# Turning the ternary down-weight pieces by DMA in place of TensorE

## The chip, the cores and the metric

The kernel runs on one core of a Trainium2 chip. The metric is the device time of one execution in microseconds (us); a kernel's time is the median of several runs. The profile is of one further execution.

## The reference

Four conditioned sequences of 1024 rows of 512 numbers pass through two layers. The first quantises its activations and its down weights:

```python
scale = cond @ norm_w.T + 1.0
h = x * (scale[:, None, :] * rsqrt(mean(x * x) + EPS))
val, gate = split(h @ up_w.T)                  # up_w: 4096 x 512
h = val * gelu(gate)                           # 2048 wide
hq = round(h * 127 / max|h|) * max|h| / 127    # per row
wq = clip(round(down_w / mean|down_w|), -1, 1) * mean|down_w|   # down_w: 512 x 2048
x1 = hq @ wq.T + x
```

The second layer is a bottleneck of 128 whose two weight matrices are built from the condition: `x1 + relu(x1 @ Wd_b.T + bd) @ Wu_b.T + bu`, with `Wd_b = Wd + 0.1 * (cond @ Wdd.T + bdd)` and `Wu_b` alike.

## The kernel before

The 4096 rows are worked in eight chunks of 512. A chunk has 16 iterations j. In each, TensorE (PE) multiplies one gate tile (12 matmuls of 128x512, three for each of four slices of the 512 inputs: high by high, high by low and low by high half of a split float, L947 to L949) and one value tile of the same size. ScalarE (ACT) applies Gelu to the gate tile (L545), VectorE (DVE) multiplies it by the value tile (L797), ScalarE takes the absolute value (L556) and VectorE a running maximum (L734). From the next chunk on, the 16 tiles of the chunk before are scaled and rounded (L706, L522, L525), and in iterations 9 to 12 PE does the down products with `wqT`, the turned ternary weights (L1000). Beside this the condition's big matrices stream through (loads L299, turned on VectorE by L724, multiplied by PE at L959). After the eight chunks the second layer follows.

Chunk 0 also prepares the weights. Every engine runs its own list of instructions in the order written, and semaphores join them. In iteration j of chunk 0:

- **SP** issues all DMAs, one after another: `load_up(j + 4)` (two loads of up weights, L278), in j = 7 and 8 `turn_x`, which turns the next chunk's rows by DMA transposes from SBUF to SBUF (L269 for the high half, L271 for the low half, each 128x512 of a 2-byte type), `load_pieces(j - 6)` for j = 7 to 13 (L292; it waits until the piece before in the same buffer is quantised), in j = 11 three loads `load_nat` of 512 KB (L299) and from j = 13 one each.
- **PE** does the gate tile (it waits for `w_lo_done`, L1023, that is, for `w_lo_half(j)` on VectorE), `turn_w(j + 2)` (8 transposes in float32 of the up weights, L924; waits for `w_scaled`), the value tile, and for j >= 8 `turn_pieces(j - 8)` (L933 to L940).
- **ACT** does Gelu(j), `w_hi_half(j + 2)` (L510), `w_square(j + 3)` (L504), the absolute value, for j = 7 to 14 the two pieces' scaling and rounding (L569), and for j >= 8 `copy_pieces(j - 8)` (L513), which converts eight turned blocks to fp8 in `wqT` (L516).
- **DVE** does the maximum of j - 1 (L734), from j = 13 a unit of `turn_nat` (L724), `w_lo_half(j + 2)` (L665), the product (L797), `w_exponents(j + 3)` (L641 to L651), `w_scale(j + 3)` (L658), and for j = 7 to 14 `quant_pieces(j - 7)`: clip both pieces (L711), wait until the pair before has been turned (L713), then write both to `piece_q`, a bfloat16 view of `s_bc` (L716).

The down weights go through in 16 pieces of 128x512, two at a time: the pair i is loaded in SP's iteration i + 6, rounded and clipped in iteration i + 7 and turned and converted in iteration i + 8. The turned blocks lie in the PSUM bank TA, whose uses are counted by `ta_full` and `ta_freed`; TA also serves the row of scales (L496). The first use of `wqT` is in chunk 1, iteration 9 (L993). With the first iteration of chunk 1 PE turns the running maximum of chunk 0 (L984, after the gate tile; it waits for all 16 maxima), and before its gate tile it waits for 15 products (`h_done`, L1019).

Of the kernel before, what the change touches and what calls it, by code (L numbers as in the profile page):

```python
# [7 lines left out]
BF16 = mybir.dt.bfloat16  # L8
# [3 lines left out]
ACT = mybir.ActivationFunctionType  # L12
AX = mybir.AxisListType

P = 128
# [7 lines left out]
def conditioned_block(nc, x, cond, norm_w, up_w, down_w, Wd, bd, Wu, bu, Wdd, bdd, Wdu, bdu, out):  # L23
# [9 lines left out]
    FT = FF // P  # L33
# [14 lines left out]
    with ExitStack() as ctx:  # L48
        def sb(name, shape, dt):
            return ctx.enter_context(nc.sbuf_tensor(name, shape, dt))  # L50

        def sem(name):
            return ctx.enter_context(nc.semaphore(name))
# [4 lines left out]
        w_hi = w_hi_reg[:, :].bitcast(F16).rearrange("p (k f) -> p k f", k=KD)  # L58
        w_lo = w_lo_reg[:, :].bitcast(F16).rearrange("p (k f) -> p k f", k=KD)
        wqT = sb("wqT", [P, FT, D], F8)  # L60
        base_wd = sb("base_wd", [P, KD * BN], F32)
        base_wu = sb("base_wu", [P, D], F32)

# [67 lines left out]
        def piece_q(p):  # L131
            return s_bc[:, :].bitcast(BF16)[:, (p % 2) * 512:(p % 2 + 1) * 512]
# [10 lines left out]
        def x_bank(k):  # L143
# [28 lines left out]
        piece_in = [sem(f"piece_in{i}") for i in range(2)]  # L172
        piece_biased, piece_quant, mean_step, base_done = (sem(n) for n in (
            "piece_biased", "piece_quant", "mean_step", "base_done"))
        x0_in = [sem(f"x0_in{t}") for t in range(TT)]
        x_in, x_squared, ms_done, x_rstd, x_scaled = sem("x_in"), sem("x_squared"), sem("ms_done"), sem("x_rstd"), sem("x_scaled")
        ta_full, ta_freed, x_hi_done, x_lo_done, x_turned = (sem(n) for n in (
# [23 lines left out]
        TA_BASE = KD  # L201
        TA_SC = TA_BASE + 2
        TA_MEAN = TA_SC + 1
        TA_PIECE = TA_MEAN + 1
        TA0 = TA_PIECE + FT // 2


        def squares_in(c, j):
# [49 lines left out]
        def _(sp):  # L258
# [26 lines left out]
            def load_pieces(i):  # L285
                for p in (2 * i, 2 * i + 1):
                    if i == 0 and p == 0:
                        sp.wait_ge(ta_full, TA_BASE + 2)
                    if i > 0:
                        sp.wait_ge(piece_quant, 4 * (i - 1) + 3 + p % 2)  # L290
                    dt, fb = p // 4, p % 4
                    sp.dma_start(piece(p), down_w[dt * P:(dt + 1) * P, fb * 512:(fb + 1) * 512]).then_inc(piece_in[p % 2], 16)  # L292

            def load_nat(u):
                m, t = u // 4, u % 4
                src = (Wdd, Wdu)[m % 2].rearrange("(a u p e) h -> u p a (e h)", a=2, p=P, e=4)[4 * (m // 2) + t]
                if u >= NAT:
                    sp.wait_ge(nat_turned, u - NAT + 1)
                sp.dma_start(nat[:, u % NAT, :, :], src).then_inc(nat_in[u % NAT], 16)  # L299
# [43 lines left out]
            def run(c, par, b):  # L343
                first, last = is_first(c), b is None
                for j in range(FT):
                    if first and j < FT - 4:
                        load_up(j + 4)
                    if not last and not first and j == 1:
                        load_x(c + 1)
                    if not last:  # L350
                        for t in turns_in(c, j):
                            turn_x(c + 1, t)
                    if last and j == 4:
                        sp.wait_ge(x_turned, 32 * TT * c)
                        load_x1(0, 0)
                        sp.wait_ge(val_full, FT * c)
                        load_x1(1, 1)
                    if first and j == 4:
                        load_rows(3)
                        load_pieces(0)  # L360
                    if first and 7 <= j < 14:
                        load_pieces(j - 6)
                    if first and j == 11:
                        for u in range(NAT):
                            load_nat(u)
                    for u in units_at(c, j):
                        if u + NAT < UNITS:
                            load_nat(u + NAT)
                    if not first:
                        if j in (7, 8):  # L370
                            load_xr(c - 1, j - 7)
                        if 10 <= j < 10 + TT:
                            store_x1(c - 1, j - 10)
                        if j in (11, 12):
                            load_xr(c - 1, j - 9)
                    for m in batch_at(c, j):
                        if m % 2 == 1:
                            store_stage(m)
                    if last and j == 6:
                        load_deltas()  # L380
# [90 lines left out]
        def _(act):  # L471
# [40 lines left out]

            def copy_pieces(i):  # L513
                dt, f0 = i // 2, 8 * (i % 2)
                act.wait_ge(ta_full, TA_PIECE + i + 1)
                act.activation(wqT[:, f0:f0 + 8, dt * P:(dt + 1) * P],  # L516
                               TA[:, :].bitcast(BF16).rearrange("p (f d) -> p f d", f=8), ACT.Copy, saturate=False).then_inc(ta_freed, 1)

            def round_pair(c, k0):
                for k in (k0, k0 + 1):  # L520
# [116 lines left out]
        def _(dve):  # L637
# [70 lines left out]
            def quant_pieces(i):  # L708
                for p in (2 * i, 2 * i + 1):
                    dve.wait_ge(piece_biased, p + 1)  # L710
                    dve.tensor_scalar(piece(p), piece(p), ROUND + 1.0, ROUND - 1.0, ALU.min, ALU.max).then_inc(piece_quant, 1)  # L711
                if i > 0:
                    dve.wait_ge(ta_full, TA_PIECE + i)  # L713
                for p in (2 * i, 2 * i + 1):
                    dve.wait_ge(piece_quant, 4 * i + 1 + p % 2)
                    dve.tensor_scalar(piece_q(p), piece(p), ROUND, None, ALU.subtract).then_inc(piece_quant, 1)  # L716
# [195 lines left out]
        def _(pe):  # L912
# [17 lines left out]
                    mm = pe.transpose(TA[:, k * P:(k + 1) * P], sc[:, k, b:b + 1].to_broadcast([P, P]), identf[:, :])  # L930
                mm.then_inc(ta_full, 1)

            def turn_pieces(i):  # L933
                pe.wait_ge(piece_quant, 4 * i + 4)
                pe.wait_ge(ta_freed, TA_PIECE + i)
                for p in (2 * i, 2 * i + 1):
                    for a in range(4):
                        o = (4 * (p % 2) + a) * P
                        mm = pe.transpose(TA[:, :].bitcast(BF16)[:, o:o + P], piece_q(p)[:, a * P:(a + 1) * P], identb[:, :])
                mm.then_inc(ta_full, 1)  # L940

            def up_products(par, ft, bank, done, x_waits=False):
                cols = slice(ft * P, (ft + 1) * P)
                for k in range(KD):
# [47 lines left out]

            def down_products(c, t):  # L993
                if t == 0:
                    pe.wait_ge(ta_freed, TA0)
                    pe.wait_ge(q_done, FT * (c + 1))
                if t > 0:
                    pe.wait_ge(y_done, TT * c + t)
                for f in range(FT):
                    mm = pe.matmul(Y[:, :], q[:, f, t * P:(t + 1) * P], wqT[:, f, :], start=(f == 0), stop=(f == FT - 1))  # L1000
                mm.then_inc(y_full, 1)
# [12 lines left out]
            def run(c, par, b):  # L1014
# [5 lines left out]
                for j in range(FT):  # L1020
# [31 lines left out]
                        spread_scales(c - 1)  # L1052
                    if row_in(c, j):
                        spread_row(b)
                    if first and j >= 8:
                        turn_pieces(j - 8)
                    if not first and 9 <= j < 9 + TT:
                        down_products(c - 1, j - 9)

# [119 lines left out]
```

## Time and profile before

| what | value |
|---|---|
| median of 3 runs | 972.29 us (970.92 to 973.04) |
| the profiled execution | 972.11 us |
| its span | 970.3 us |
| PE busy | 952.5 us (98%) |
| DVE busy | 667.7 us (69%) |
| ACT busy | 432.3 us (45%) |
| granted TensorE clock, mean over the span | 0.998 |
| DMA queues, share of 16 engines | 48.9% |

The profiled execution lies 0.18 us under the median, and what lies around its span is 1.8 us. "Busy" counts the time in which an engine executes; a matmul of 128x512 is shown as 380 ns, but the next begins 0.22 us after it, so neighbours overlap.

### The profile page before, as it was taken

The page shows a single profiled execution, that of the slowest core. Times are in us where ns is not written, and L with a number is a line of the kernel's source. Part 1 is how long each engine was busy: PE and PEld are TensorE (multiplying, and loading weights), DVE is VectorE, ACT ScalarE, POOL GpSimd, SP SyncE. Part 2 cuts the span into 40 slices and gives each one's busy share as a digit, 9 for nine tenths or more (in the row PEclk, how much of TensorE's full clock was granted, in tenths as well). Part 3 has the DMA queues.
Part 4 walks back from the last instruction along what each step waited for, and adds up shares of the span by engine and source line. Part 5 has one row for each costly group of instructions (what it writes and reads, how often), then busy time and mean ns, then how long its engine had stood idle before and what let it go on. Part 6 is the DMA issues. An engine that isn't in the chain of part 4 may idle for free.

```text
span 970.3 us, 13569 instructions
## 1 busy us (share of the span) xinstructions
PE 952.5 (98%) x5248; PEld 456.0 (47%) x5248; DVE 667.7 (69%) x1053; ACT 432.3 (45%) x795; POOL 52.1 (5%) x52
## 2 busy tenths in 40 slices
PE   7999999999999999999999999999999999999998
PEld 5545544444444444444444444444444444445453
DVE  6769877866877577857886687857787584236333
ACT  5778767322752157213742266214741265117121
POOL 1000000000000000000000000000000000000554
PEclk9999999999999999999999999999999999999999
DMA  9445543564436643573347643764346632210674
GB/s 328 149 136 169 176 151 98 150 186 113 160 109 175 172 131 98 152 194 127 119 129 177 150 132 101 176 163 141 120 141 154 162 131 72 81 55 22 237 239 175
DMA packets 103769, 141.93 MB, mean 146 GB/s; under 512 B 35732, under 2 KB 41368, under 8 KB 103192
## 3 DMA queue, kind: packets, MB, share of 16 engines
q1 hardware_dynamic: 103704, 141.06, 48.9%
q8 instruction: 41, 0.67, 0.3%
q14 instruction: 24, 0.20, 0.1%
HBM read 112.72 MB, written 20.97 MB: 138 GB/s over the span
## 4 chain that ended last, share of the span: by engine, by line
PE 94%; DVE 2%; DMA 2%; ACT 1%; issue 1%; SPq 0%; DVEq 0%; ACTq 0%
PE bank L947 22%; PE bank L948 22%; PE bank L949 22%; PE bank L1000 10%; PE bank L959 6%; PE bank L1121 3%; PE bank L1134 3%; DMA xn<-in_x 2%; PE bank L1010 1%; PE bank L1112 1%; PE bank L924 1%; PE bank L984 0%; PE bank L990 0%; DVE h L797 0%; ACT h L576 0%
## 5 line engine op out<-in xcount | busy, mean ns | idle before, releaser
L947 PE MATMUL bank<-x_split,w_hi 128*128 128x512 f16 x1024 | 389.1, 380 | 2.3 <-DVE x_split L676 2.3
L948 PE MATMUL bank<-x_split,w_hi 128*128 128x512 f16 x1024 | 388.9, 380 | 0.0
L949 PE MATMUL bank<-x_split,w_lo 128*128 128x512 f16 x1024 | 388.7, 380 | 0.0
L724 DVE STREAM_TRANSPOSE delta_reg<-delta_reg 128x512 f32<-128x512 f32 x256 | 261.0, 1110 | 12.9 <-PE bank L959 12.9
L556 ACT ACTIVATE g<-h 128x512 f32<-128x512 f32 x128 | 80.7, 630 | 271.2 <-DVE h L797 271.2
L797 DVE SCALAR_TENSOR_TENSOR h<-bank,desc,g 128x512 f32<-128x512 f32 x128 | 94.5, 738 | 113.1 <-issue 88.9
L545 ACT ACTIVATE g<-bank,desc 128x512 f32<-128x512 f32 x128 | 87.7, 685 | 164.0 <-PE bank L949 163.8
L947 PEld LDWEIGHTS bank<-x_split,w_hi 128*128 128x128 f16 x1024 | 100.4, 98 | 128.3 <-issue 11.1
L949 PEld LDWEIGHTS bank<-x_split,w_lo 128*128 128x128 f16 x1024 | 100.4, 98 | 121.2 <-issue 0.7
L948 PEld LDWEIGHTS bank<-x_split,w_hi 128*128 128x128 f16 x1024 | 100.4, 98 | 112.1 <-issue 0.8
L1000 PE MATMUL bank<-wqT,qreg 128*128 128x512 fp8e4 x448 | 101.3, 379 | 0.0
L734 DVE TENSOR_TENSOR absrun<-absrun,g 128x512 f32<-128x512 f32 x120 | 82.4, 686 | 24.5 <-ACT g L556 23.7
L706 DVE TENSOR_TENSOR h<-h,s_bc 128x512 f32<-128x512 f32 x112 | 71.7, 681 | 2.0 <-ACT s_bc L529 2.0
L1000 PEld LDWEIGHTS bank<-wqT,qreg 128*128 128x128 bf16 x448 | 43.8, 98 | 52.9
L752 DVE SCALAR_TENSOR_TENSOR xr<-bank,fy,xr 128x512 f32<-128x512 f32 x30 | 22.4, 751 | 66.5 <-DMA xr<-in_x 28.6
L522 ACT ACTIVATE h<-h 128x512 f32<-128x512 f32 x112 | 64.4, 621 | 5.3 <-DVE h L706 5.3
L525 ACT ACTIVATE qreg<-h 128x512 bf16<-128x512 f32 x112 | 63.6, 616 | 0.0
L959 PE MATMUL bank<-delta_reg,cond_diag 128*32 128x256 f32 x1024 | 61.9, 382 | 0.0
L888 DVE TENSOR_TENSOR w_hi<-bank,w_hi 128x512 f32<-128x512 f32 x32 | 21.9, 690 | 39.9 <-PE bank L1134 39.6
L446 POOL TENSOR_TENSOR rstd<-ss,mhalf 128x4 f32<-128x4 f32 x8 | 10.7, 1334 | 691.3 <-DVE ss L670 691.3
L959 PEld LDWEIGHTS bank<-delta_reg,cond_diag 128*32 128x32 f32 x1024 | 30.0, 109 | 30.0 <-issue 13.6
L1134 PE MATMUL bank<-delta_reg,w_lo 128*128 128x512 f32 x64 | 30.5, 609 | 1.3 <-ACT w_lo L608 0.8
(133 smaller groups left out, 558.1 us busy)
## 6 DMA issues: line engine op xcount, KB each, us to landing
delta_reg<-in_L_cond_Wdd SPq DMA_DIRECT2D x64, 512.0 KB, 3.8
delta_reg<-in_L_cond_Wdu SPq DMA_DIRECT2D x64, 512.0 KB, 3.8
qreg<-in_L_cond_up_w SPq DMA_DIRECT2D x32, 256.0 KB, 4.3
xr<-in_x SPq DMA_DIRECT2D x30, 256.0 KB, 4.3
x_scratch<-xr SPq DMA_DIRECT2D x30, 256.0 KB, 4.7
xn<-in_x SPq DMA_DIRECT2D x7, 1024.0 KB, 6.3
out_y<-w_hi SPq DMA_DIRECT2D x7, 1024.0 KB, 4.8
h<-in_L_cond_down_w SPq DMA_DIRECT2D x4, 1024.0 KB, 7.9
```

What stands on the lines that cost most here:

```text
L522: act.activation(h[:, k, :], h[:, k, :], ACT.Copy, bias=ROUND).then_inc(round_added, 1)
L545: act.activation(g[:, j % 2, :], GATE[j % 2][:, :], ACT.Gelu, scale=desc[:, 2 * j + 1:2 * j + 2]).then_inc(gelu_done, 1)
L556: act.activation(g[:, j % 2, :], h[:, j, :], ACT.Abs).then_inc(abs_done, 1)
L706: dve.tensor_tensor(h[:, k, :], h[:, k, :], s_bc[:, :], ALU.mult).then_inc(h_scaled, 1)
L724: last = dve.transpose(natT[:, t, kk, :, :].rearrange("p a (r e) -> p e a r", e=4), nat[:, u % NAT, kk, :])
L734: dve.tensor_tensor(absrun[:, :], absrun[:, :], g[:, j % 2, :], ALU.max).then_inc(max_done, 1)
L797: dve.scalar_tensor_tensor(h[:, j, :], VAL[j % 2][:, :], desc[:, 2 * j:2 * j + 1], g[:, j % 2, :], ALU.mult, ALU.mult).then_inc(h_done, 1)
L947: pe.matmul(bank[:, :], w_hi[:, k, cols], xh[:, par, k, :], start=(k == 0), stop=False)
L948: pe.matmul(bank[:, :], w_hi[:, k, cols], xl[:, par, k, :], start=False, stop=False)
L949: mm = pe.matmul(bank[:, :], w_lo[:, k, cols], xh[:, par, k, :], start=False, stop=(k == KD - 1))
L959: mm = pe.matmul(HY[32 * t:32 * t + 32, cols], cond_diag[:, a, :], natT[:, (4 * m + t) % NATT, :, a, :], start=(a == 0), stop=(a == HB - 1))
L1000: mm = pe.matmul(Y[:, :], q[:, f, t * P:(t + 1) * P], wqT[:, f, :], start=(f == 0), stop=(f == FT - 1))
```

## The change

The eight PE instructions of each `turn_pieces(i)` are taken out of PE's list. In their place SP issues, in its iteration i + 8, ahead of `load_pieces`, two DMA transposes, each of one 128x512 bfloat16 piece from `piece_q` into the new SBUF buffer `pieceT` (2 KB a partition). They wait for the pieces to be quantised and, from the second pair on, for ScalarE to have converted the pair before (`wq_done`), as `pieceT` holds one pair. ScalarE's conversion reads `pieceT` in place of TA and waits for both transposes. VectorE's wait in `quant_pieces`, with which it spares `piece_q` until it has been read, is now for the transposes to have landed. The uses of TA are renumbered.

```diff
--- before.py
+++ after.py
@@ -58,6 +58,7 @@
         w_hi = w_hi_reg[:, :].bitcast(F16).rearrange("p (k f) -> p k f", k=KD)
         w_lo = w_lo_reg[:, :].bitcast(F16).rearrange("p (k f) -> p k f", k=KD)
         wqT = sb("wqT", [P, FT, D], F8)
+        pieceT = sb("pieceT", [P, 2, 4, P], BF16)
         base_wd = sb("base_wd", [P, KD * BN], F32)
         base_wu = sb("base_wu", [P, D], F32)
 
@@ -172,6 +173,7 @@
         piece_in = [sem(f"piece_in{i}") for i in range(2)]
         piece_biased, piece_quant, mean_step, base_done = (sem(n) for n in (
             "piece_biased", "piece_quant", "mean_step", "base_done"))
+        piece_turned, wq_done = sem("piece_turned"), sem("wq_done")
         x0_in = [sem(f"x0_in{t}") for t in range(TT)]
         x_in, x_squared, ms_done, x_rstd, x_scaled = sem("x_in"), sem("x_squared"), sem("ms_done"), sem("x_rstd"), sem("x_scaled")
         ta_full, ta_freed, x_hi_done, x_lo_done, x_turned = (sem(n) for n in (
@@ -201,8 +203,7 @@
         TA_BASE = KD
         TA_SC = TA_BASE + 2
         TA_MEAN = TA_SC + 1
-        TA_PIECE = TA_MEAN + 1
-        TA0 = TA_PIECE + FT // 2
+        TA0 = TA_MEAN + 1
 
 
         def squares_in(c, j):
@@ -290,6 +291,13 @@
                         sp.wait_ge(piece_quant, 4 * (i - 1) + 3 + p % 2)
                     dt, fb = p // 4, p % 4
                     sp.dma_start(piece(p), down_w[dt * P:(dt + 1) * P, fb * 512:(fb + 1) * 512]).then_inc(piece_in[p % 2], 16)
+
+            def turn_pieces(i):
+                for p in (2 * i, 2 * i + 1):
+                    sp.wait_ge(piece_quant, 4 * i + 3 + p % 2)
+                    if i > 0:
+                        sp.wait_ge(wq_done, i)
+                    sp.dma_start(pieceT[:, p % 2, :, :], piece_q(p), transpose=True).then_inc(piece_turned, 16)
 
             def load_nat(u):
                 m, t = u // 4, u % 4
@@ -358,6 +366,8 @@
                     if first and j == 4:
                         load_rows(3)
                         load_pieces(0)
+                    if first and j >= 8:
+                        turn_pieces(j - 8)
                     if first and 7 <= j < 14:
                         load_pieces(j - 6)
                     if first and j == 11:
@@ -512,9 +522,9 @@
 
             def copy_pieces(i):
                 dt, f0 = i // 2, 8 * (i % 2)
-                act.wait_ge(ta_full, TA_PIECE + i + 1)
+                act.wait_ge(piece_turned, 32 * (i + 1))
                 act.activation(wqT[:, f0:f0 + 8, dt * P:(dt + 1) * P],
-                               TA[:, :].bitcast(BF16).rearrange("p (f d) -> p f d", f=8), ACT.Copy, saturate=False).then_inc(ta_freed, 1)
+                               pieceT[:, :, :, :].rearrange("p a f d -> p (a f) d"), ACT.Copy, saturate=False).then_inc(wq_done, 1)
 
             def round_pair(c, k0):
                 for k in (k0, k0 + 1):
@@ -710,7 +720,7 @@
                     dve.wait_ge(piece_biased, p + 1)
                     dve.tensor_scalar(piece(p), piece(p), ROUND + 1.0, ROUND - 1.0, ALU.min, ALU.max).then_inc(piece_quant, 1)
                 if i > 0:
-                    dve.wait_ge(ta_full, TA_PIECE + i)
+                    dve.wait_ge(piece_turned, 32 * i)
                 for p in (2 * i, 2 * i + 1):
                     dve.wait_ge(piece_quant, 4 * i + 1 + p % 2)
                     dve.tensor_scalar(piece_q(p), piece(p), ROUND, None, ALU.subtract).then_inc(piece_quant, 1)
@@ -930,15 +940,6 @@
                     mm = pe.transpose(TA[:, k * P:(k + 1) * P], sc[:, k, b:b + 1].to_broadcast([P, P]), identf[:, :])
                 mm.then_inc(ta_full, 1)
 
-            def turn_pieces(i):
-                pe.wait_ge(piece_quant, 4 * i + 4)
-                pe.wait_ge(ta_freed, TA_PIECE + i)
-                for p in (2 * i, 2 * i + 1):
-                    for a in range(4):
-                        o = (4 * (p % 2) + a) * P
-                        mm = pe.transpose(TA[:, :].bitcast(BF16)[:, o:o + P], piece_q(p)[:, a * P:(a + 1) * P], identb[:, :])
-                mm.then_inc(ta_full, 1)
-
             def up_products(par, ft, bank, done, x_waits=False):
                 cols = slice(ft * P, (ft + 1) * P)
                 for k in range(KD):
@@ -992,7 +993,7 @@
 
             def down_products(c, t):
                 if t == 0:
-                    pe.wait_ge(ta_freed, TA0)
+                    pe.wait_ge(wq_done, FT // 2)
                     pe.wait_ge(q_done, FT * (c + 1))
                 if t > 0:
                     pe.wait_ge(y_done, TT * c + t)
@@ -1052,8 +1053,6 @@
                         spread_scales(c - 1)
                     if row_in(c, j):
                         spread_row(b)
-                    if first and j >= 8:
-                        turn_pieces(j - 8)
                     if not first and 9 <= j < 9 + TT:
                         down_products(c - 1, j - 9)
```

## Rows read from the trace of the kernel before

**Rows 1.** Page, part 1 (busy us, share, instructions) and part 4 (chain).

```profile
PE 952.5 (98%) x5248; PEld 456.0 (47%) x5248; DVE 667.7 (69%) x1053; ACT 432.3 (45%) x795; POOL 52.1 (5%) x52
...
PE 94%; DVE 2%; DMA 2%; ACT 1%; issue 1%; SPq 0%; DVEq 0%; ACTq 0%
```

**Rows 2.** Busy time by stretch: start:end length, busy us by engine, granted clock, DMA.

```profile
131.00:250.00 119.00, 119.00 (x698) 54.74 (x696) 89.40 (x121) 52.05 (x93) 1.38 (x1) 1.00 0.49 143
```

**Rows 3.** Chain that ended last, 80 to 90 us: start, us, what.

```profile
81.13 0.45 PE bank L939 x8
```

**Rows 4.** Timeline of SP's queue, 78 to 107 us: start, us, engine, line, what.

```profile
78.63 0.81 SPq L292 DMA_DIRECT2D qreg<-in_L_cond_down_w  x2
79.49 0.90 SPq L278 DMA_DIRECT2D qreg<-in_L_cond_up_w  x2
...
81.68 1.26 SPq L271 DMA_TRANSPOSE x_split<-xn  x1
...
84.30 1.26 SPq L271 DMA_TRANSPOSE x_split<-xn  x1
85.61 1.05 SPq L292 DMA_DIRECT2D qreg<-in_L_cond_down_w  x2
...
105.14 1.46 SPq L299 DMA_DIRECT2D delta_reg<-in_L_cond_Wdd  x3
```

**Rows 5.** Single DMAs by source line: issue in ns, start; then issue to landing.

```profile
L271 SPq DMA_TRANSPOSE x_split<-xn x1: 1264/1264/1264, 81.7 to 81.7; - x1
...
DMA to landing us min/median/max: 3.7/3.7/3.7
...
L271 SPq DMA_TRANSPOSE x_split<-xn x1: 1264/1264/1264, 84.3 to 84.3; - x1
...
DMA to landing us min/median/max: 2.5/2.5/2.5
...
L299 SPq DMA_DIRECT2D delta_reg<-in_L_cond_Wdd x2: 469/469/469, 105.6 to 106.1; - x2
...
DMA to landing us min/median/max: 5.8/6.2/6.6
```

**Rows 6.** Timeline of DVE, 84 to 124 us.

```profile
84.86 0.76 DVE L716 TENSOR_SCALAR s_bc<-qreg 128x512 bf16<-128x512 f32 x2
...
92.81 1.29 DVE L665 TENSOR_TENSOR w_lo<-bank,w_hi 128x512 f16<-128x512 f32 x2 [0.27 <-ACT w_hi L510]
...
95.76 0.88 DVE L658 TENSOR_SCALAR qreg<-qreg,winv 128x512 f32<-128x512 f32 x2
96.56 0.76 DVE L711 TENSOR_SCALAR qreg<-qreg 128x512 f32<-128x512 f32 x2
...
110.23 0.76 DVE L716 TENSOR_SCALAR s_bc<-qreg 128x512 bf16<-128x512 f32 x2
...
123.64 0.76 DVE L716 TENSOR_SCALAR s_bc<-qreg 128x512 bf16<-128x512 f32 x2
```

**Rows 7.** Timeline of ACT, 84 to 91 us.

```profile
84.39 1.00 ACT L516 ACTIVATE wqT<-bank 128x1024 fp8e4<-128x1024 bf16 x1
...
90.71 1.00 ACT L516 ACTIVATE wqT<-bank 128x1024 fp8e4<-128x1024 bf16 x1
```

**Rows 8.** Timeline of PE, 66 to 130 us.

```profile
69.56 1.09 PE L924 MATMUL bank<-identf,qreg 128*128 128x128 f32 x8 [2.30 <-DVE qreg L658]
...
128.90 0.66 PE L984 MATMUL bank<-identf,absrun 128*128 128x128 f32 x4 [0.98 <-DVE absrun L734]
```

**Rows 9.** Busy time by stretch, the stretch after PE stood at 67 to 69.6 us.

```profile
70.60:74.26 3.66, 3.66 (x12) 1.35 (x11) 3.66 (x7) 3.53 (x8) 0.00 (x0) 0.53 0.19 40
```

**Rows 10.** Page, part 5: 128x512 reads by ScalarE, from SBUF and from PSUM.

```profile
L556 ACT ACTIVATE g<-h 128x512 f32<-128x512 f32 x128 | 80.7, 630 | 271.2 <-DVE h L797 271.2
...
L545 ACT ACTIVATE g<-bank,desc 128x512 f32<-128x512 f32 x128 | 87.7, 685 | 164.0 <-PE bank L949 163.8
```

**Rows 11.** Transposes of L269 over the whole span, issue to landing.

```profile
DMA to landing us min/median/max: 2.5/5.1/6.3
```

## Prediction

> **What bounds the kernel now.** I read the page first: PE is busy 98% of the span and makes up 94% of the chain that ended last [rows 1]. Then the busy time by stretch: from 131 to 250 us PE never stops, at full clock [rows 2]. So what starts PE late at the end of chunk 0 is not made up later; a delay there is a delay of the end. The chain from 80 to 90 us shows the instructions in question on that chain: eight transposes of L939 hold PE for 0.45 us [rows 3]. Last I read the queues beside PE in iterations 8 to 15 of chunk 0, since the change moves the work to SP and puts waits of ScalarE and VectorE behind it. Four readings matter. SP issues without a gap from 79.49 to 86.66 us, a DMA transpose taking 1.26 us of its time [rows 4]. VectorE was ready to write the second pair of pieces at 84.86 us [rows 6], ScalarE to convert the first at 84.39 us [rows 7]. And PE waits there for VectorE's scaled up weights and, at the change of chunk, for its last maximum [rows 8].
>
> **PE's share.** 8 times 0.45 us [rows 3] go, 3.6 us at most. That is what the change can win, if everything else stays hidden. It counts only while PE is what ends last.
>
> **The first pair.** SP reaches `turn_pieces(0)` behind the four transposes of x, at 85.61 us, where `load_pieces(2)` stood [rows 4]. The second transpose is issued at 85.61 + 1.26 = 86.87. The nearest row for its landing is the one issued at 84.30, with no loads ahead of it: 2.5 us [rows 5]. It lands at 89.4. VectorE stands at L713 from 84.86 to 89.4, 4.5 us, and behind this wait are the low halves of the up weights, the product and `w_scale`, which PE needs for its next `turn_w`. ScalarE stands at `copy_pieces(0)` from 84.39 to 89.4, and behind it are the next Gelu and `w_hi_half`. Neither has anything else to do first, so PE stops as well. The 0.45 us that PE saves in each iteration become waiting: from here on my sum follows L716, not PE.
>
> **The loop that then forms.** Landing of pair i - 1, VectorE's first L716 (half of 0.76 us [rows 6], with its signal 0.45), `load_pieces`, `load_up`, two transposes, landing of pair i. The same sequence stands in the trace, with transposes of x: pieces issued at 78.63, up weights at 79.49, the second transpose at 81.68 [rows 4], landed 3.7 us later [rows 5], so 85.38 - 78.63 = 6.75 us from the loads to the landing. The loop takes 6.75 + 0.45 = 7.2 us. The engines' own loop runs from the conversion (90.71 [rows 7]) over w_lo at 92.81 and w_scale at 95.76 to the end of the clipping at 96.56 + 0.76 [rows 6], 6.6 us. 7.2 is the longer, so it is the period for iterations 9, 10 and 11: 89.4, 96.6, 103.8, 111.0 us.
>
> **Iteration 12.** Between its `load_pieces` and `turn_pieces(4)` stand the three 512 KB loads, 1.46 us of issue [rows 4]. The last one landed at 106.1 + 6.6 = 112.7, which is 8.4 us after the piece load at 104.30 [rows 4, 5]. In the sequence of the last part the transposes landed right behind the loads issued ahead of them, so I put the pair 0.5 us behind these: 0.45 + 8.9 = 9.35 us, 120.35 in place of 110.23 [rows 6], 10.1 us late.
>
> **Iterations 13 and 14.** The up weights are finished. The two intervals take 13.4 us before (110.23 to 123.64 [rows 6]); I leave the first as it is, for its transposes follow only the pieces, and add 0.8 us to the second, where one 512 KB load is ahead again (as much data as in the 7.2 us loop). Bounds: nothing, and 2 us. L716 of the last pair: 134.5 in place of 123.64, 10.9 us late. What follows up to PE's turn of the maximum is unchanged: 128.90 [rows 8] becomes 139.8. The last conversion (pair 7) waits for a pair issued at about 135.5, landed about 139.3; it ends behind PE's turn and has chunk 1 to be read in, so it costs nothing.
>
> **ScalarE's conversion.** It keeps its shape and 1.00 us [rows 7], only the source moves from PSUM to SBUF. Of 128x512 the pass from SBUF takes 630 ns, one from PSUM 685 (another function) [rows 10]: between 0.1 us less and 0.1 us more. I take nothing; it lies in the 6.6 us loop, which has 0.6 us to spare.
>
> **The clock.** PE will stand at the end of chunk 0 for over 5 us: its own work would be done by 134, and the maximum comes at 139.8. Before, PE stood for 2.30 us [rows 8], and the 3.66 us that began 1 us after it resumed were granted 0.53, about the lower level of 1.2 GHz [rows 9]. That is 3.66 x 0.47 = 1.7 us lost. After the 0.98 us stop at 128.90 [rows 8] the clock stayed whole. The stop of over 5 us is on PE's path and gets the 1.7 us; the earlier drops fall into waiting time and cost nothing. Bounds: nothing, and twice as much.
>
> **The sum.** 10.9 + 1.7 = 12.6 us. PE's 3.6 us are not subtracted, as they are inside the waits. Against the profiled execution of 972.11 us (span 970.3) this gives 984.7; the median of the runs shown is 0.18 us higher, so 984.9 us.
>
> **A rule beside the rows.** Eight transposes in 0.45 us are 56 ns each on PE [rows 3], and a DMA transpose of four such blocks lands after 2.5 us alone [rows 5]. The Trainium skill, "VectorE: DVE Perf Modes", section "The three transpose paths", gives 390 ns for a 128x128 bf16 transpose on TensorE and 1309 ns through the DMA crossbar. It speaks against the change as I do, but by its figures 64 blocks would free 25 us of PE and a pair of pieces would take 10.5 us to turn; no row here has blocks that slow on either path.
>
> **Rivals.**
> (a) Faster. The mechanism: the pairs land before VectorE and ScalarE come to their waits, and PE's path shrinks by 3.6 us, to 968.7. The place that decides is the first pair: it would have to be issued by 82.4 us to land by 84.86. For it: VectorE and ScalarE are not the bound. Against: SP is held by the x transposes up to 85.61 [rows 4], and nothing in the change moves them. 3 in 100; that waits and gain cancel, 2 in 100.
> (b) The first stop happens, but the loop keeps up. If transposes don't queue behind loads, the second lands 0.85 + 0.9 + 1.26 + 2.5 = 5.5 us after the loads, the loop is 6.0, and the engines' 6.6 sets the period: 89.4 + 3 x 6.6 = 109.2, and the same for iteration 12, 115.8; 5.6 us late. Without the clock's cost 977.9, with it 979.6. Against: in chunk 0 the transpose behind loads took 3.7 us, not 2.5 [rows 5]. 15 in 100.
> (c) The transposes queue worse than in the nearest row. Over the span the median to landing is 5.1 us and the worst 6.3 [rows 11], among the 512 KB loads. With 5.1 in place of 3.7 in each of three loops and one like it for iteration 14, 5.6 us more, 990.5; with 6.3 it is 995. 12 in 100.
> (d) The two transposes of a pair go one after the other instead of overlapping. With 3.7 us each the loop is 0.45 + 1.75 + 7.4 = 9.6; the first pair lands at 85.61 + 5.0 = 90.6, and six loops later it is 148.2 in place of 123.64: 24.6 + 1.7 late, 998.6. Against: transposes issued 1.3 us apart landed well under twice that [rows 4, 5]. 3 in 100. By the 1309 ns of the Trainium skill, "VectorE: DVE Perf Modes", "The three transpose paths", a pair would take 10.5 us, which is this case made sharper: a loop of 12.7 us and a time of some 1020 us.
> The forecast itself has 65 in 100.
>
> **The numbers.** The forecast spreads from 981 to 989 by its bounds (the 3 us of iteration 12, iteration 14, the clock). With most of (b) below and the start of (c) above, 978 to 990 holds 8 in 10. A measurement of this kernel tells about 0.2%, 1.9 us, from no change: faster has 0.03, within it 0.02, slower 0.95.
>
> **What would show it.** First, the first L716 of the second pair: at 89.4, waiting on the DMA into `pieceT`. Second, the intervals between pairs of L716: 7.2, 7.2, 7.2, 9.3 us, and the waits of L516 for the same DMA of about 5 us, then some 0.5 to 3. Third, L984 at 139.8 and a clock of about 0.5 for some 3.5 us behind it. Fourth, from then on every row later by one constant. If L716 comes at 84.9 the first step is wrong; if the intervals are 6.6, it is (b); if L984 is at 125 to 129, it is (a), and I have misjudged the whole direction. If the delay is some 11 us at L984 but less at the end, then PE was not the bound behind it.

## The result and the profile after

| | kernel before | changed kernel |
|---|---|---|
| median | 971.61 us (4 runs, 970.79 to 973.04) | 988.03 us (4 runs, 986.91 to 989.32) |
| profiled execution | 972.11 us, span 970.3 | 988.77 us, span 986.9 |

The ratio is 1.0168, with a 95% interval of 1.0156 to 1.0181: 16.4 us slower. The forecast was 984.9 us, that is 12.6 us slower, within 978 to 990. The lines of the changed kernel are numbered a little higher: L716 is now L726 (`piece_q`), L516 is L526 (ScalarE's conversion), L924 is L934 (`turn_w`), L984 is L985 (the turn of the maximum), L990 is L991 (the turn of the scales), L292 and L278 are L293 and L279 (loads of pieces and of up weights), L299 is L307 (the 512 KB loads), and L300 are the new transposes.

The page of the changed kernel, parts 1 and 4, beside [rows 1]:

```profile
PE 957.7 (97%) x5184; PEld 456.5 (46%) x5184; DVE 667.8 (68%) x1053; ACT 433.1 (44%) x795; POOL 52.1 (5%) x52
...
PE 90%; DVE 3%; DMA 3%; SPq 2%; issue 1%; ACT 1%; DVEq 0%; ACTq 0%
PE bank L948 21%; PE bank L949 21%; PE bank L950 21%; PE bank L1001 10%; PE bank L960 6%; PE bank L1120 3%; PE bank L1133 3%; DMA pieceT<-s_bc 2%; PE bank L1011 1%; PE bank L1111 1%; PE bank L934 1%; SPq L300 1%; DVE w_lo L675 0%; DVE h L80
```

PE is busy for longer in total although 64 instructions are gone (in this stage it ran at the lower clock in two stretches, near 95 and near 143 us, below), and the new DMA is 2% of the chain that ended last. The chain between 84 and 98 us (start, us, what) is the mechanism, link by link:

```profile
84.69 1.27 SPq L272
...
86.01 1.26 SPq L300
...
87.32 2.48 DMA pieceT<-s_bc
...
89.82 0.04 DVE s_bc L726
...
90.65 0.43 SPq L293
...
91.12 0.43 SPq L279
...
92.14 1.19 SPq L300
...
93.43 3.83 DMA pieceT<-s_bc
...
97.28 0.04 DVE s_bc L726
```

SP's transposes of x, then the two new ones, then the landing, then the first write of `piece_q`; this releases the load of the next pieces, behind which come the up weights, the next two transposes and the next landing. No matmul stands in it. SP's timeline, for the first two pairs and for the pair behind the three 512 KB loads, beside [rows 4]:

```profile
86.01 2.57 SPq L300 DMA_TRANSPOSE pieceT<-s_bc  x2
90.28 0.80 SPq L293 DMA_DIRECT2D qreg<-in_L_cond_down_w  x2
91.12 0.90 SPq L279 DMA_DIRECT2D qreg<-in_L_cond_up_w  x2
92.14 2.52 SPq L300 DMA_TRANSPOSE pieceT<-s_bc  x2
...
112.21 0.81 SPq L293 DMA_DIRECT2D qreg<-in_L_cond_down_w  x2
113.07 1.46 SPq L307 DMA_DIRECT2D delta_reg<-in_L_cond_Wdd  x3
114.62 3.50 SPq L300 DMA_TRANSPOSE pieceT<-s_bc  x2
```

VectorE's timeline, the first `piece_q` of a pair each time, beside [rows 6]; in brackets how long it was idle before and for what. The line at 104.01 is the clipping of pair 3:

```profile
89.82 0.76 DVE L726 TENSOR_SCALAR s_bc<-qreg 128x512 bf16<-128x512 f32 x2 [4.48 <-DMA pieceT<-s_bc]
...
97.28 0.76 DVE L726 TENSOR_SCALAR s_bc<-qreg 128x512 bf16<-128x512 f32 x2 [1.01 <-DMA pieceT<-s_bc]
...
101.67 0.75 DVE L807 SCALAR_TENSOR_TENSOR h<-bank,desc,g 128x512 f32<-128x512 f32 x1 [0.95 <-issue]
...
104.01 0.77 DVE L721 TENSOR_SCALAR qreg<-qreg 128x512 f32<-128x512 f32 x2
104.82 0.76 DVE L726 TENSOR_SCALAR s_bc<-qreg 128x512 bf16<-128x512 f32 x2
...
111.76 0.76 DVE L726 TENSOR_SCALAR s_bc<-qreg 128x512 bf16<-128x512 f32 x2 [0.49 <-DMA pieceT<-s_bc]
...
122.54 0.76 DVE L726 TENSOR_SCALAR s_bc<-qreg 128x512 bf16<-128x512 f32 x2 [4.34 <-DMA pieceT<-s_bc]
```
```profile
137.42 0.76 DVE L726 TENSOR_SCALAR s_bc<-qreg 128x512 bf16<-128x512 f32 x2 [1.40 <-DMA pieceT<-s_bc]
```

In the second interval (97.28 to 104.82) VectorE doesn't wait for the landing: its clipping ended at 104.78, and the chain that ended last has the landing at 104.80. It had stood 0.95 us before its product (L807), of which the profile names no cause; PE worked at the lower clock on the value tile that this product reads. So here the landing and the engines' own work ended together.

Who waited for the new transposes (us in all, times), and their issue to landing over all 16:

```profile
  ACT wqT L526: 15.1, 7
  DVE s_bc L726: 11.7, 5
...
DMA to landing us min/median/max: 2.5/3.8/7.4
```

PE's timeline where it stood longest, beside [rows 8], and the busy time, with the granted clock third from the end of the line, beside [rows 9]:

```profile
95.25 1.97 PE L934 MATMUL bank<-identf,qreg 128*128 128x128 f32 x8 [4.65 <-DVE qreg L668]
```
```profile
142.65 1.12 PE L985 MATMUL bank<-identf,absrun 128*128 128x128 f32 x4 [6.12 <-DVE absrun L744]
...
148.58 0.60 PE L991 MATMUL bank<-identf,s 128*128 128x128 f32 x4
```
```profile
142.65:150.00 7.35, 7.35 (x25) 3.65 (x26) 3.39 (x8) 1.99 (x3) 0.00 (x0) 0.60 0.43 134
```

PE stood for 4.65 us near 95 and for 6.12 us before the turn of the maximum, and in the 7.35 us that followed it had 0.60 of the clock: the first matmuls there start 0.43 us apart, as at the lower level, 1.2 GHz, in place of 0.22. From the turn of the maximum to the turn of the scales it took 5.93 us (142.65 to 148.58), where the kernel before needed 3.08 (128.90 to 131.98), of which the second line is

```profile
131.98 0.60 PE L990 MATMUL bank<-identf,s 128*128 128x128 f32 x4
```

So the 16.6 us by which the spans differ are these, counted from the first L716 or L726 (78.18 before, 78.58 after). Two lines of the kernel before on which the intervals rest:

```profile
78.18 0.76 DVE L716 TENSOR_SCALAR s_bc<-qreg 128x512 bf16<-128x512 f32 x2
...
103.85 0.76 DVE L716 TENSOR_SCALAR s_bc<-qreg 128x512 bf16<-128x512 f32 x2
```

| piece | before | after | lost, us | forecast, us |
|---|---|---|---|---|
| start of the span to the first pair | 78.18 | 78.58 | 0.40 | 0 |
| interval to pair 1 (iteration 8) | 6.68 | 11.24 | 4.56 | 4.5 |
| pairs 2, 3 and 4 (iterations 9 to 11) | 18.99 | 21.94 | 2.95 | 2.6 |
| pair 5 (iteration 12, 512 KB loads) | 6.38 | 10.78 | 4.40 | 3.0 |
| pairs 6 and 7 | 13.41 | 14.88 | 1.47 | 0.8 |
| last pair to the turn of the maximum | 5.26 | 5.23 | 0.0 | 0 |
| turn of the maximum to turn of the scales | 3.08 | 5.93 | 2.85 | 1.7 |
| from there to the end | 838.3 | 838.3 | 0.0 | 0 |

### The profile page after: what moved, and what is told of

Read it like the earlier page. It is cut to its first block, busy times and chain, and to the rows that moved or that the text cites. A ratio compares the mean times of both kernels' runs of the same rounds, so it can differ in the third digit from the quotient of the medians.

```text
span 986.9 us, 13463 instructions
## 1 busy us (share of the span) xinstructions
PE 957.7 (97%) x5184; PEld 456.5 (46%) x5184; DVE 667.8 (68%) x1053; ACT 433.1 (44%) x795; POOL 52.1 (5%) x52
## 4 chain that ended last, share of the span: by engine, by line
PE 90%; DVE 3%; DMA 3%; SPq 2%; issue 1%; ACT 1%; DVEq 0%; ACTq 0%
PE bank L948 21%; PE bank L949 21%; PE bank L950 21%; PE bank L1001 10%; PE bank L960 6%; PE bank L1120 3%; PE bank L1133 3%; DMA pieceT<-s_bc 2%; PE bank L1011 1%; PE bank L1111 1%; PE bank L934 1%; SPq L300 1%; DVE w_lo L675 0%; DVE h L807 0%; DMA xn<-in_x 0%
## 5 line engine op out<-in xcount | busy, mean ns | idle before, releaser
L807 DVE SCALAR_TENSOR_TENSOR h<-bank,desc,g 128x512 f32<-128x512 f32 x128 | 94.5, 738 | 111.0 <-issue 86.6
L716 DVE TENSOR_TENSOR h<-h,s_bc 128x512 f32<-128x512 f32 x112 | 71.8, 683 | 4.4 <-ACT s_bc L539 4.4
L532 ACT ACTIVATE h<-h 128x512 f32<-128x512 f32 x112 | 64.4, 622 | 5.3 <-DVE h L716 5.3
```

Source lines behind the costliest of these rows:

```text
L532: act.activation(h[:, k, :], h[:, k, :], ACT.Copy, bias=ROUND).then_inc(round_added, 1)
L716: dve.tensor_tensor(h[:, k, :], h[:, k, :], s_bc[:, :], ALU.mult).then_inc(h_scaled, 1)
L807: dve.scalar_tensor_tensor(h[:, j, :], VAL[j % 2][:, :], desc[:, 2 * j:2 * j + 1], g[:, j % 2, :], ALU.mult, ALU.mult).then_inc(h_done, 1)
```

## The experiments

The theory: the time is lost because VectorE and ScalarE wait for a landing of their own iteration, in a loop that runs through SP's queue; the slow clock after the long stop comes on top; and PE's freed 3.6 us are worth up to 3.6 us. The main rival: SP's 20 us of added issue time and the added traffic cost it, whoever waits. A second one: ScalarE's wait alone makes the loop. "To the maximum" is the time from the first L716 to the turn of the maximum, in the profile of each. The ratio is to the runs of the kernel before that were made beside each kernel; their medians lie between 971.2 and 972.3 us.

| kernel | median us | ratio to before, 95% interval | to the maximum | on to the scales |
|---|---|---|---|---|
| before | 971.6 | 1 | 50.7 | 3.1 |
| changed kernel | 988.0 | 1.0168 (1.0156 to 1.0181) | 64.1 | 5.9 |
| both buffers doubled | 975.6 | 1.0043 (1.0028 to 1.0058) | 54.2 | 3.1 |
| `piece_q` doubled | 985.7 | 1.0146 (1.0131 to 1.0161) | 60.8 | 5.9 |
| `pieceT` doubled | 988.4 | 1.0174 (1.0159 to 1.0189) | 64.4 | 5.7 |
| no turning | 975.7 | 1.0049 (1.0032 to 1.0066) | 52.3 | 4.8 |
| before, with idle transposes | 974.7 | 1.0032 (1.0022 to 1.0042) | 53.5 | 3.1 |
| first pair ahead | 988.0 | 1.0164 (1.0149 to 1.0180) | 65.0 | 5.2 |
| PE kept busy | 984.7 | 1.0127 (1.0112 to 1.0143) | 63.9 | 3.1 |
| 512 KB loads later | 985.3 | 1.0129 (1.0110 to 1.0148) | 61.3 | 5.7 |
| no turning, nobody waits | 972.8 | 1.0010 (1.0001 to 1.0020) | 49.6 | 4.6 |
| the same, PE kept busy | 972.5 | 1.0004 (0.9994 to 1.0013) | 50.7 | 3.0 |
| both doubled, x spread | 974.3 | 1.0025 (1.0014 to 1.0036) | 52.4 | 4.8 |
| the same, PE kept busy | 973.2 | 1.0014 (1.0005 to 1.0024) | 52.3 | 3.0 |

### The waits: both buffers doubled

A second pair of `piece_q` and a second `pieceT` lie in a part of `delta_reg` that nobody uses before chunk 1 (whose first writer waits for the last conversion). Each pair parity has a semaphore of its own.

```diff
-                if i > 0:
-                    dve.wait_ge(piece_turned, 32 * i)
+                if i > 1:
+                    dve.wait_ge(piece_turned[i % 2], 32 * (i // 2))
...
-                    if i > 0:
-                        sp.wait_ge(wq_done, i)
+                    if i > 1:
+                        sp.wait_ge(wq_done, i - 1)
...
-                    if first and j >= 8:
-                        copy_pieces(j - 8)
+                    if first and j >= 9:
+                        copy_pieces(j - 9)
+                    if c == 1 and j == 0:
+                        copy_pieces(7)
```

> The changed kernel with two pairs of piece_q and two of pieceT, the conversion one iteration later: nobody waits for a transpose of the same iteration. My theory (the time is lost in the waits of VectorE and ScalarE for a landing of the same iteration): PE's 3.6 us come through and at most 1 us of loads issued late is lost, 968.0 to 969.5. Rival (SP's queue time and the transposes' traffic cost it): both are still there, so 980 or more.

975.6 us: 12.5 of the 16.4 us are gone with the waits, though every DMA is still issued. But 4 us remain, and the theory's 968.0 to 969.5 is missed by 6 us. ScalarE's timeline in this kernel shows the first of them:

```profile
91.42 0.72 ACT L591 ACTIVATE qreg<-qreg,wtot 128x512 f32<-128x512 f32 x1 [2.33 <-DMA qreg<-in_L_cond_down_w]
93.05 0.72 ACT L591 ACTIVATE qreg<-qreg,wtot 128x512 f32<-128x512 f32 x1 [0.91 <-DMA qreg<-in_L_cond_down_w]
```

It waits 2.33 and 0.91 us for the pieces of pair 2 (L591 is its L569). SP had issued them at 88.19, behind four x transposes and two new ones, where the kernel before issued them at 85.61 [rows 4]. So the rival holds a part: the place in SP's queue.

### The queue and the traffic alone: idle transposes

The kernel before, PE turning as ever, with 16 DMA transposes of spare memory at the places of the new ones.

```diff
+            def idle_turn(i):
+                for p in (2 * i, 2 * i + 1):
+                    sp.wait_ge(piece_quant, 4 * i + 3 + p % 2)
...
+                    sp.dma_start(idle_out[:, p % 2, :, :], idle_in, transpose=True).then_inc(idle_turned[p % 2], 16)
...
+                    if first and j >= 8:
+                        idle_turn(j - 8)
                     if first and 7 <= j < 14:
                         load_pieces(j - 6)
```

> The kernel before, PE still turning, with the changed kernel's 16 DMA transposes at the same places of SP's queue but from and into spare memory, with nobody waiting for them (each only for the one into its place an iteration ago). My theory (waits): SP's 20 us of issue and the traffic cost at most 1.5 us, 971.5 to 973. Rival (queue and traffic): 980 or more.

974.7 us, 3.1 more (interval of the ratio 1.0022 to 1.0042), and 2.8 us more up to the maximum. Twice the 1.5 us that the theory allowed, and well below the rival's 980. The cause is in the same place, ScalarE's wait for pair 2 (L584 is its L569):

```profile
90.19 0.72 ACT L584 ACTIVATE qreg<-qreg,wtot 128x512 f32<-128x512 f32 x1 [2.35 <-DMA qreg<-in_L_cond_down_w]
92.10 0.72 ACT L584 ACTIVATE qreg<-qreg,wtot 128x512 f32<-128x512 f32 x1 [1.20 <-DMA qreg<-in_L_cond_down_w]
```

So SP's queue and the traffic cost about 3 us up to the maximum when nobody waits for a transpose. Of the 13.4 us that the changed kernel loses up to there, 10 go with the waits (54.2 in place of 64.1 us with both buffers doubled). How the two overlap in the changed kernel is taken up below.

### Which wait closes the loop

`piece_q` doubled only: VectorE may run a pair ahead, ScalarE still waits for this iteration's landing.

```diff
-                if i > 0:
-                    dve.wait_ge(piece_turned, 32 * i)
+                if i > 1:
+                    dve.wait_ge(piece_turned, 32 * (i - 1))
```

> The changed kernel with two pairs of piece_q only: VectorE waits for the pair before the last, ScalarE still for this iteration's. My theory: the first stop of 4.9 us stays at ScalarE, the loads are no longer held by a landing, so the loop shrinks from 7.4 to 6.7; with iteration 12's 2 us and the clock 980 to 984. Rival (ScalarE's wait alone makes the loop): no change from 988.

`pieceT` doubled only, with the conversion one iteration later: VectorE still waits.

```diff
-                    if i > 0:
-                        sp.wait_ge(wq_done, i)
+                    if i > 1:
+                        sp.wait_ge(wq_done, i - 1)
...
+                    if first and j >= 9:
+                        copy_pieces(j - 9)
```

> The changed kernel with two pairs of pieceT and the conversion one iteration later, one pair of piece_q: only VectorE waits for a landing of the same iteration. My theory: the loop landing, piece_q, load_pieces, load_up, transposes, landing is untouched, 7.2 to 7.5 us, so 986 to 988. Rival (ScalarE's wait alone makes the loop): 970 or less.

985.7 and 988.4 us. Taking away ScalarE's wait changes nothing; taking away VectorE's gives 2.3 us back, where the theory had 4 to 8, and is 1.7 us outside my range. The waits of the first kernel, then of the second (us in all, times, longest):

```profile
DVE w_lo L676 <- ACT w_hi L521: 10.6, 5, 5.4
ACT wqT L527 <- DMA pieceT<-s_bc: 9.7, 4, 4.9
...
PEld bank L988 <- DVE absrun L747: 4.9, 1, 4.9
...
ACT wqT L527 <- DMA pieceT<-delta_reg: 4.4, 3, 2.4
```
```profile
ACT g L579 <- DVE h L824: 26.4, 9, 7.7
DVE s_bc L741 <- DMA pieceT<-s_bc: 11.8, 4, 4.6
...
PEld bank L1002 <- DVE absrun L761: 6.6, 1, 6.6
...
DVE s_bc L741 <- DMA delta_reg<-s_bc: 3.4, 2, 1.7
```

With VectorE free, ScalarE is the one that stands before the landing (9.7 us for the pairs that lie in `s_bc`, 4.4 for those in `delta_reg`), and VectorE then stands for ScalarE's high half (10.6). With ScalarE free, VectorE stands (11.8 and 3.4), and ScalarE for its product (26.4). VectorE's wait alone keeps the whole loss, ScalarE's alone 14 of the 16.4 us, and the 12.5 us of the kernel with both buffers doubled come only with both removed. That ScalarE's wait is the only one that matters is refuted by `pieceT` doubled.

### The first stop

```diff
+                    if first and j == 8:
+                        turn_pieces(0)
                     if not last:
                         for t in turns_in(c, j):
                             turn_x(c + 1, t)
...
-                    if first and j >= 8:
+                    if first and j >= 9:
                         turn_pieces(j - 8)
```

> The changed kernel with the first pair's transposes ahead of the four x transposes of iteration 8. My theory: the first stop falls from 4.5 to about 1 us, but the x transposes then hold load_pieces(2) until 88.5 in place of 90.28, so 1.8 us of it stay gained: 986.2. Rival (the first stop is absorbed later anyway): 988.

988.0 us: nothing gained, the rival's number. But it is not absorbed: VectorE's first interval fell from 11.24 to 7.00 us, as meant, and the next rose from 7.46 to 12.04. The x transposes, pushed back, ran into the loads of pair 2 (issued at 87.08, while VectorE's data were ready at 84.5), and the second transpose of pair 1 landed after 5.6 us, where it took 3.8 in the changed kernel. That one transpose, issue and landing:

```profile
L300 SPq DMA_TRANSPOSE pieceT<-s_bc x1: 1222/1222/1222, 90.5 to 90.5; - x1
...
DMA to landing us min/median/max: 5.6/5.6/5.6
```

Here a place in SP's full queue was only handed on.

### Iteration 12

The three 512 KB loads come behind `turn_pieces(4)` and ahead of `load_pieces(6)` in iteration 12.

```diff
-                    if first and j == 11:
-                        for u in range(NAT):
-                            load_nat(u)
...
                     if first and j >= 8:
                         turn_pieces(j - 8)
+                    if first and j == 12:
+                        for u in range(NAT):
+                            load_nat(u)
```

> The changed kernel with the three 512 KB loads of iteration 11 moved behind the transposes of pair 4 in iteration 12. My theory: the interval of iteration 12 falls from 10.8 to 6.6 us and up to 1 us comes back in the next, 984 to 985. Rival (the engines need the 10.8 us): 988.

985.3 us, just above the 984 to 985 expected. The interval of that iteration fell from 10.78 to 6.37 us, as expected (the engines need no more), and the turn of the maximum comes 2.8 us sooner. That is not the whole 4.4: the intervals of pairs 2 to 4, which lie ahead of the edit, were 1.3 us longer in this execution than in the changed kernel's, which I take for a difference between executions (in PE kept busy, the same code up to there, they were 0.4 us longer), and pair 6's was 0.3 us longer behind it.

### The clock

```diff
+                        if c == 1:
+                            keep_busy(110)
                         turn_absrun(c - 1)
```

with `keep_busy(n)` n matmuls of 128x128 into the free bank Y.

> The changed kernel with 110 small matmuls into a free bank between PE's first gate tile of chunk 1 and its turn of the maximum, where it stands for 6.1 us. My theory: the clock stays whole and the 2.9 us that the slow stretch costs come back, 985.1. Rival (the clock is low for another reason than the stop): 988 or more.

984.7 us, against 985.1 expected, and from the maximum to the scales 3.08 us again. The stop itself is the cause of the slow stretch; it costs 2.85 us by the two profiles.

### What PE's share is worth

No turning at all: ScalarE converts `piece_q` as it lies. The down weights are so in the wrong order, and the down product is not the reference's.

```diff
-                    if first and j >= 8:
-                        turn_pieces(j - 8)
...
-                act.wait_ge(piece_turned, 32 * (i + 1))
+                act.wait_ge(piece_quant, 4 * (i + 1))
...
-                               pieceT[:, :, :, :].rearrange("p a f d -> p (a f) d"), ACT.Copy, saturate=False).then_inc(wq_done, 1)
+                               s_bc[:, :].bitcast(BF16).rearrange("p (f d) -> p f d", f=8), ACT.Copy, saturate=False).then_inc(wq_done, 1)
...
-                    dve.wait_ge(piece_turned, 32 * i)
+                    dve.wait_ge(wq_done, i)
```

> The pieces are not turned at all: no transposes by PE or DMA, ScalarE converts piece_q as it lies (the weights of the down product are so in the wrong order). It measures what PE's 64 transposes were worth. My theory: PE is the bound in these iterations, 971.6 - 3.6 = 968.0. Rival (PE has slack there): 971 to 972.

975.7 us, slower than before by 4.5 although no work was added. Neither theory had that. In the profiled execution 1.6 us of it came up to the maximum, 1.7 between it and the scales, and 1.2 at the very end, behind VectorE's last instruction, of which these runs name no cause. The experiment has a wait of its own (VectorE for ScalarE's conversion, 3.6 us in seven pieces), so it was made again with two pairs of `piece_q`, and then with PE kept busy:

```diff
-                if i > 0:
-                    dve.wait_ge(wq_done, i)
+                if i > 1:
+                    dve.wait_ge(wq_done, i - 1)
```

> As the kernel without any turning (weights in the wrong order), with two pairs of piece_q, so that VectorE no longer waits 3.6 us for ScalarE's conversions: now nothing but PE's 64 transposes is missing from the kernel before. Theory now: VectorE and ScalarE set the last maximum of chunk 0, so PE's 3.6 us become a longer stop before it, which costs up to 1.7 us of clock: 971.5 to 973.5. Rival (my step in the prediction, PE's path shrinks by 3.6 us): 968.

> The same with 70 small matmuls ahead of PE's turn of the maximum in chunk 1, which hold the clock. Theory now: at most the 0.98 us by which PE waited there before can be won and the clock stays whole, 970.5 to 971.5. Rival (PE's path): 968 or, if the small matmuls take their place, 972.

972.8 and 972.5 us, against 972.0 for the kernel before beside them. PE's timeline in the first, before the turn of the maximum and after:

```profile
128.10 1.11 PE L990 MATMUL bank<-identf,absrun 128*128 128x128 f32 x4 [2.76 <-DVE absrun L749]
...
132.73 0.60 PE L996 MATMUL bank<-identf,s 128*128 128x128 f32 x4
```

The turn of the maximum comes 1.2 us sooner (49.6 in place of 50.7 us from the first L716), not 3.6: PE now waits there 2.76 us in place of 0.98. And the longer stop costs the clock, 4.63 us to the turn of the scales in place of 3.08. In the second kernel the 70 small matmuls held the clock (3.03) but ended 1.0 us after VectorE's last maximum, so the maximum was turned at 50.7 as before. Its 972.5 us miss the 970.5 to 971.5 expected and are what the rival gave for small matmuls that take the place of the turning, so this kernel decides nothing between the two. The first one does: PE's path did not shrink by 3.6 us, and the rival's 968 is out. With the turning free of charge the change wins 1.2 us and the clock takes 1.5. With the clock held by matmuls of the right length some 1 us would stay won, an estimate from the profiles' 49.6 and 3.0 us; no run here shows it.

### Can both kernels be beaten?

Both buffers doubled, and one of the two x row tiles of iteration 8 turned in iteration 9; then PE kept busy with 70 small matmuls as well.

```diff
-            return [t for t, a in enumerate((7, 7, 8, 8) if is_first(c) else (10, 11, 12, 13)) if a == j]
+            return [t for t, a in enumerate((7, 7, 8, 9) if is_first(c) else (10, 11, 12, 13)) if a == j]
```

> The kernel with two pairs of both buffers and the conversion an iteration later, with the x transposes of one of the two row tiles of iteration 8 moved to iteration 9. Theory: the 3.4 us that kernel lost at iteration 9 came from load_pieces(2), issued 2.6 us late behind six transposes; with four ahead it is issued in time, so 971.5 to 974 with the clock's cost. Rival (traffic of the transposes, not their place in the queue): 975 or more.

> The same with 70 small matmuls ahead of PE's turn of the maximum. Theory: 971 to 972, level with the kernel before, since PE's share is worth nothing. Rival (PE's path): 968 to 969.

974.3 and 973.2 us, 0.3 and 1.2 us above what the theory allowed; the rival's 975 or more is missed too. Pair 2 was now loaded in time (at 85.29), but pair 3 was late in its turn (issued at 93.42, 15.1 us after the load of pair 1, where before it was 13.0), and its interval is 8.32 us in place of 6.05. The second kernel lies 0.14% above the one before (0.05 to 0.24%). Its 70 small matmuls too ended 1.0 us after the last maximum; without that it would be at some 972.2 us, an estimate, against 972.0 for the kernel before. None of the kernels measured here beats the kernel before.

## Why the prediction was right, and where it was off

**The direction and the mechanism held.** The first L726 that waits came at 89.82, forecast 89.4; of the difference 0.40 us lie ahead of the first pair in this execution. The working of the first pair (SP free at 85.6, 1.26 us of issue, 2.5 us of landing) reads in the chain above term by term. Rival (a), faster, had no case: even with the turning removed the kernel is not faster (972.8 against 972.0 us).

**The loop** was put at 7.2 us and measured 7.46, 7.54 and 6.94. The landing behind piece and up loads was 3.8, 3.9 and 2.9 us, put at 3.7. Rival (d), a loop of 9.6, is refuted by these intervals. Rival (b) rested on a landing of 2.5 us behind the loads and an engine-bound loop of 6.6; it is refuted by the landings, and by the waits of 1.01 and 0.49 us for them in the first and the third interval. The second interval is no clean case: there the engines' own work, slowed after the stop near 95 us, took as long as the landing. The prediction let the earlier slow stretches fall into waiting time at no cost; in this interval that only just held. The 16 new transposes, of four 128x128 blocks each, landed after 2.5 us at the least and 3.8 in the median. The Trainium skill, "VectorE: DVE Perf Modes", section "The three transpose paths", has 1309 ns for one such block through the crossbar. Four in a row would by that figure be 5.2 us, an estimate, and the trace doesn't agree.

**Iteration 12 was undersized.** Forecast 9.35 us, measured 10.78. Two terms: the first transpose behind the 512 KB loads was issued in 2.03 us instead of 1.2, and the second landed 5.8 us after its issue began at 116.8. By the forecast it would have been down 8.9 us after the loads of the pieces began; it took 10.3 (112.21 to 122.5). The moved loads confirm the place and the size: 6.37 us without them in front.

**The pair behind one 512 KB load**, forecast 0.8 us, with a bound of 2: pairs 6 and 7 lost 1.47.

**The clock term was undersized**, 1.7 us forecast and 2.85 measured, inside its bounds. That the stop costs it is shown by PE kept busy. I took the length of the slow stretch from the stop of 2.30 us (3.66 us). After 6.12 us the slow stretch lasted until the turn of the scales, 5.7 us, and it began with the first matmul, not 1 us later.

These add up: 0.06 for the first stop, 0.35 for the loop, 1.4, 0.7 and 1.15, with the 0.4 at the start, are the 4 us between 12.6 and 16.6.

**The step that was wrong in substance** is "PE's share". I wrote that 3.6 us is what the change can win, and read it from the chain of the kernel before, where L939 stood with 0.45 us. That each instruction stands on the chain says only that PE was the last by a little in these iterations. At the end of chunk 0 PE waited 0.98 us for VectorE's maximum [rows 8] already, and that row was in my hands: what ended last there was not PE, so only that part of its saving counts by which VectorE's maximum comes sooner. Without the turning that was 1.2 us, while PE's wait grew from 0.98 to 2.76, and 1.5 us of clock stood against it. The 0.98 us is no bound for the gain either, as my expectation for no turning with PE kept busy had it. In the sum this did no harm, since I had set PE's gain to nothing, but rival (a) priced it at 968.7, and two of my expectations at 968 to 969.5.

**Left out of the sum** was what the queue does to others: `load_pieces(2)` is issued 2.6 us late even when nobody waits for a transpose, which costs about 3 us by the idle transposes. In the changed kernel this is hidden in the same stop, so it doesn't add; it shows only when the waits are gone. That the stop and the queue delay overlap in this way is argued from the intervals, not tested by itself.

## What to carry to other kernels

Before work is moved from a busy engine to a DMA queue, look for who will wait for its landing in the same iteration, and through which other loads the wait closes into a loop; here a landing of some 4 us, in a loop with issue times of 1.2 us and single buffers, made intervals of 7 to 7.5 us out of 6.3, and of two waits for it each alone kept 14 us or more of the 16.4. An engine at 98% need not be worth its whole saving: the row in which it waits for a second engine at the end of the stage is the warning, and here 1.2 of 3.6 us came through. And a longer stop of TensorE has a price of its own in the clock behind it.

## What had not been expected

- After PE's stops in this stretch the granted clock differed for like lengths. A stop of 2.76 us (no turning, nobody waits) was followed by a slow stretch that cost 1.5 us; one of 2.8 us at the same place, with both buffers doubled, by none (3.08 us to the scales, granted clock 1.00), and one of 3.13 us there, with x spread as well, again by one that cost 1.7 us. What PE had done before was different in them, and what of it decides is open.
- Most DMA transposes of the changed kernel occupied SP's queue for 1.19 to 1.29 us. The two behind three 512 KB loads took 2.03 and 1.37 us. Such loads are not needed for it: with both doubled and x spread, a transpose at 91.2 us, the fourth in a row behind the loads of pieces and up weights, took 2.19 us.
- ScalarE's conversion from SBUF took 1.06 us, from PSUM 1.00 [rows 7]: the SBUF side was the slower one, against the sign of [rows 10], by too little to matter.
